# A decoder layer on one core: all steps ordered by a string of letters, first expert tiles in three parts, routing batch by batch

## What is computed

```python
x = _layernorm(x + _attn(x, x, x, ..., True), ln1_g, ln1_b)
x = _layernorm(x + _attn(x, encoder_output, encoder_output, ..., False), ln2_g, ln2_b)
x = _layernorm(x + _moe(x, router_w, router_b, e_w1, e_b1, e_w2, e_b2), ln3_g, ln3_b)
# _attn
scores = jnp.einsum('bqhd,bkhd->bhqk', Q, Kp) / jnp.sqrt(jnp.float32(HD))
a = jax.nn.softmax(scores, axis=-1)
o = jnp.einsum('bhqk,bkhd->bqhd', a, V).reshape(Bq, Sq, Dm)
# _moe
topw, topi = jax.lax.top_k(softmax(xf @ rw + rb), K)
h = gelu(einsum('td,edf->etf', xf, w1) + b1[:, None, :], approximate=False)
out = einsum('etd,te->td', einsum('etf,efd->etd', h, w2) + b2[:, None, :], combine)
```

## Time and profile before

| | |
|---|---|
| median of three runs | 1112.58 us (1112.13 to 1116.31) |
| the profiled execution: time, span | 1113.5 us, 1111.8 us |
| TensorE matmuls busy | 1020.5 us, 92% |
| ScalarE, VectorE, GpSimd busy | 588.8 us, 562.8 us, 306.6 us |
| mean granted TensorE clock | 0.971 |
| chain that ended last: TensorE, ScalarE, VectorE, DMA | 80%, 6%, 5%, 4% |

### The profile page before, as it was taken

The page is one execution under the profiler, slowest core; times in us unless marked ns, Lnnn a source line. Parts: engine busy times, 40 slices in busy tenths (PEclk is TensorE's granted clock), DMA queues, the critical chain, the costliest instruction groups (busy, mean ns, idle before and its releaser), DMA issues.

```text
span 1111.8 us, 19112 instructions
## 1 busy us (share of the span) xinstructions
PE 1020.5 (92%) x6320; PEld 593.4 (53%) x6321; DVE 562.8 (51%) x922; ACT 588.8 (53%) x1201; POOL 306.6 (28%) x416
## 2 busy tenths in 40 slices
PE   5899799999999999999999999996688899999976
PEld 3445445334336534344433333322678899999965
DVE  3542566876665767766775766842231121121126
ACT  2264363776765676766566666664233344433462
POOL 7633622405104712103233022361022011111114
PEclk9899999999999999999999999999789899999988
DMA  8634222004105202103503021021112053125134
GB/s 226 162 100 123 66 70 78 20 1 116 30 2 132 69 2 58 30 2 101 174 2 86 1 58 29 20 92 53 53 48 84 13 194 123 49 90 182 43 101 141
DMA packets 71650, 83.98 MB, mean 76 GB/s; under 512 B 10657, under 2 KB 65185, under 8 KB 71457
## 3 DMA queue, kind: packets, MB, share of 16 engines
q1 hardware_dynamic: 66080, 65.79, 20.9%
q0 software_dynamic: 5504, 17.34, 4.6%
HBM read 38.89 MB, written 12.36 MB: 46 GB/s over the span
## 4 chain that ended last, share of the span: by engine, by line
PE 80%; ACT 6%; DVE 5%; DMA 4%; issue 2%; SPq 2%; POOL 1%; ACTq 0%; POOLq 0%; DVEq 0%
PE o_bank L1057 15%; PE v_slot L1470 11%; PE a_bank L1042 11%; PE v_slot L1015 9%; PE a_bank L1462 9%; PE a_bank L983 6%; ACT probs L1170 4%; PE a_bank L998 3%; PE v_slot L1019 3%; PE o_bank L1462 3%; DVE max_q L1227 3%; PE v_slot L1079 2%; DMA inputs<-slots_in 2%; PE v_slot L1065 1%; PE v_slot L1020 1%
## 5 line engine op out<-in xcount | busy, mean ns | idle before, releaser
L1227 DVE TENSOR_REDUCE max_q<-v_slot 128x1 f32<-128x1024 f32 (+3 forms) x352 | 398.5, 1171 | 152.6 <-PE v_slot L1015 90.1
L1170 ACT ACTIVATE probs<-a_bank 128x512 f32<-128x512 f32 (+1 forms) x688 | 361.7, 592 | 176.7 <-PE a_bank L1042 115.8
L1042 PE MATMUL a_bank<-q_stack_cross,k_stack_cross 99*128 99x512 bf16 x512 | 165.7, 384 | 5.8 <-ACT probs L1170 4.0
L1476 ACT ACTIVATE hidden<-a_bank,b 128x128 f32<-128x128 f32 x216 | 79.2, 367 | 160.5 <-PE a_bank L1462 149.0
L1015 PE MATMUL v_slot<-k_stack_cross,q_stack_cross 96*128 96x512 bf16 x512 | 152.0, 382 | 4.0 <-DVE max_q L1227 2.9
L1057 PE MATMUL o_bank<-probs,v_cross 128*32 128x512 f32 x1024 | 136.4, 604 | 6.0 <-ACT probs L1170 3.2
L1462 PE MATMUL a_bank<-x_col,stack_or_weights 128*128 128x128 f32 x864 | 114.4, 285 | 18.7 <-ACTq L1192 15.7
L1470 PE MATMUL v_slot<-stack_or_weights,hidden 128*128 128x256 f32 x576 | 130.3, 379 | 0.0
L1462 PEld LDWEIGHTS a_bank<-x_col,stack_or_weights 128*128 128x128 f32 x864 | 110.6, 201 | 21.1 <-ACTq L1192 16.1
L1042 PEld LDWEIGHTS a_bank<-q_stack_cross,k_stack_cross 99*128 99x128 bf16 x512 | 46.5, 97 | 136.7 <-ACT probs L1170 89.7
L1470 PEld LDWEIGHTS v_slot<-stack_or_weights,hidden 128*128 128x128 f32 x576 | 106.6, 190 | 13.0
(11 more groups left out here) (237 smaller groups left out, 1153.4 us busy)
## 6 DMA issues: line engine op xcount, KB each, us to landing
stack_or_weights<-in_e_w SPq DMA_DIRECT2D x16, 1024.0 KB, 7.7
stack_or_weights<-parts SPq DMA_DIRECT2D x96, 128.0 KB, 2.4
k_stack_cross<-parts SPq DMA_DIRECT2D x96, 128.0 KB, 2.4
q_stack_cross<-parts SPq DMA_DIRECT2D x48, 128.0 KB, 2.4
inputs<-in_ctxT POOLq DMA_DIRECT2D x4, 1024.0 KB, 7.3
y_got<-token_out SPq DMA_DIRECT2D x16, 256.0 KB, 6.2
x_slots<-slots_in SPq DMA_DIRECT2D x30, 129.0 KB, 2.1
inputs<-in_xT POOLq DMA_DIRECT2D x4, 512.0 KB, 4.7
```

Of the source, the lines that this page charges most:

```text
L1042: last = nc.tensor.matmul(bank[:, i * cols:(i + 1) * cols], lhs, q_stack[kind][0:KM, G * u + j, q0:S], start=True, stop=bool(kind))
L1170: nc.scalar.activation(probs[tile % 2][:, js[0]:js[-1] + 1, q0:S], a_bank[at % AS][:, 0:len(js) * (S - q0)].rearrange("p (j t) -> p j t", ...
L1227: nc.vector.tensor_reduce(most, rows, X, ALU.max, negate=True).then_inc(v_free, 1)
L1476: nc.scalar.activation(hidden[:, f, :], h_bank[f % HB][:, 0:P], ACT.Gelu, bias=b1[:, bass.ds(e * FC + f, 1)]).then_inc(flow.gelu_done, 1)
```

## The change

1. The planner is gone. `STEPS`, a string of 1448 letters, says of which chain the next step is taken (w weigh, o o_turn, e score, m max or max_rows, r rows_in, a k v s c the chains of projections, loads and norms). The steps themselves are the same, except for routing.
2. Routing (`choose`, `place`) is done for each batch alone, in one scratch tile; `scatter` of a batch follows its `place`, one behind each `weigh`. Only batch 2's eight are left where 24 were.
3. The early tiles are in three parts: the first expert's but the last tile (behind `norm`), that last tile (behind `route`), and the second expert's (behind `rank`). `early_tiles_i` counts whole tiles, at least two. `choose` of batch 3 runs at once behind its logits; what counts the tiles stands behind the second expert's first tile; the wait for the last early store stands behind the first rows of flow `main`.
4. SyncE loads the weights that are needed later (`more_loads`) behind the first four splits, with `b1` among them; `b2` stays behind the early rows. The padding rows share memory with `y_self` and are made on GpSimd (`pads`) late. The last cross norm's gamma and beta go to GpSimd.

```diff
+STEPS = (
+    "aavavammmmmmkammmrkmmammkvememrmemeeemwmeeemeweawwmmmreemeemeemeewmeeweweemeweraeaeweeoeeweweweeeoeoeeweeemmwmememwwmoasm"
...
+    "wocccccc")
...
+            if b < B - 1:
+            c_chain += [("choose", b), ("place", b)]
...
+        if ev == ("split", 0, 3):
+            spread.append(("more_loads",))
+        if ev == ("max_parts", 3):
+            spread.append(("add_bias", 0))
+        if ev[0] == "place":
+            rows += [("scatter", ev[1] * QT + t, k) for t in range(QT) for k in range(2)]
+        if ev[0] == "weigh" and rows:
+            spread.append(rows.pop(0))
...
+    for step, behind in ((("pads",), ("choose", B - 2)), (("first_row",), ("att_turn", B - 1, 1)), (("experts", 0), ("norm", B - 1, 1)), (("experts", 1), ("route", B - 1)),
+                         (("rank",), ("experts", 1)), (("experts", 2), ("rank",))):
...
             sp.wait_ge(v_free, NO.v["o_turn", len(UNIT_LIST) - 1] + 1)
-            sp.dma_start(b1[:, :], a["e_b1"]).then_inc(moe_const, 16)
             sp.dma_start(b2[:, :, :], a["e_b2"].rearrange("(o e) n -> o e n", o=1).to_broadcast([P, E, D])).then_inc(moe_const, 16)
...
-                    if e == 0:
+                    part = ev[1]
+                    if part == 0:
                         sc.wait_ge(early_ready, 1)
-                        sc.wait_ge(moe_const, 32)
+                        sc.wait_ge(b1_in, 16)
...
-                        dve.wait_ge(moe_const, 32)
+                        dve.wait_ge(moe_const, 16)
 
                         dve.wait_ge(v_free, NO.v["out", B - 1, 1] + 1)
                         dve.sem_inc(early.y_evac, 1)
-                    expert_tiles(dve, early, e, lambda g, i: finish_tile(dve, early, e, g))
+                    if part < 2:
+                        early_part(dve, part, lambda g: finish_tile(dve, early, expert_of(part), g))
+                    else:
+
+                        finish_tile(dve, early, 1, first_of_second(dve))
+                        count_tiles(dve)
+                        early_part(dve, 3, lambda g: finish_tile(dve, early, 1, g))
...
+            dve.wait_ge(early.y_evac, count + 1)
+            dve.sem_inc(main.y_evac, 1)
             dve.wait_ge(early.row_ready, count + 2)
-            dve.wait_ge(early.y_evac, count + 1)
-            dve.wait_ge(early.y_stored, count * 16)
-            dve.sem_inc(main.y_evac, 1)
             copy_row(dve, main, 0)
             copy_column(dve, main, 0)
             copy_row(dve, main, 1)
+            dve.wait_ge(early.y_stored, count * 16)
```

More of the change, by code:

```diff
@@ L402, in place @@
-        if k == "split" and ev[2] == 9:
-            self.held["o_t"] = None
-    def flush_sp(self, now):
-        left = []
-        for ready, ev in sorted(self.todo_sp, key=lambda x: x[0]):
-            guard = 0.0
-            b, kind, u = UNIT_LIST[ev[1]]
-            if b:
-                guard = self.done.get(("weigh", UNIT_NO[b - 1, kind, u], key_tiles(kind) - 1))
-            if guard is None or max(ready, guard) > now:
-                left.append((ready, ev))
-                continue
-            self.order.append(ev)
-            self.done[ev] = self.use("sp", max(ready, guard), 700) + ROWS_LAND
-        self.todo_sp = left
@@ L420, in step @@
-    def step(self):
-        now = self.free["pe"]
-        self.flush_sp(now)
-        heads = []
-        for name, track in self.tracks.items():
-            i = self.at_head[name]
-            if i < len(track):
-                ready = self.needs(track[i])
-                if ready is not None:
-                    heads.append((name, track[i], ready))
-        if not heads:
-            times = [max(r, 0.0) for r, _ in self.todo_sp]
-            assert times, ("nothing can follow", self.order[-5:])
-            self.free["pe"] = max(now, min(t for t in times if t > now) if any(t > now for t in times) else now + 500)
-            return
-        first = min(max(r, now) for _, _, r in heads)
-        near = [h for h in heads if max(h[2], now) <= first + self.SOON]
-        name, ev, ready = min(near, key=self.rank)
-        self.at_head[name] += 1
-        self.place(ev, ready)
@@ L467 @@
-ORDER = Planner().build()
+            if n == UNIT_NO[B - 1, 0, UNITS - 1] and kt == QT - 1:
+                order.append(("experts_in",))
+            if kt == key_tiles(UNIT_LIST[n][1]) - 1:
+                order.append(("o_out", n))
+        elif k == "stats" and ev[2] == 0 and ev[1] + 1 < B:
+            order.append(("load_res", ev[1] + 1))
+        elif k == "norm" and ev[2] == 0 and ev[1] + 1 < B:
+            order.append(("add_bias", ev[1] + 1))
+    assert all(at[letter] == len(track) for letter, track in tracks.items())
@@ L470 @@
+    return order
+ORDER = in_order()
 class Numbers:
@@ L907, in attention_gpsimd @@
                     nc.gpsimd.tensor_tensor(rstd[:, :], rstd[:, :], neg_half[:, :], ALU.pow).then_inc(rstd_ready, 1)
-                elif k == "norm" and not on_vector(*ev[1:]):
+                elif k == "norm":
                     b, kind = ev[1:]
@@ L1372, in decoder_layer @@
         prob_step = sb("prob_step", [P, TT])
-        gelu_warm = sb("gelu_warm", [P, 1])
         top_w = sb("top_w", [P, 2, TT])
```

564 lines of the change are left out of this document (171 added, 393 removed).

## The result

| | before | after |
|---|---|---|
| median of 5 runs each, us | 1112.58 | 1048.88 |
| profiled execution, us | 1113.50 | 1043.74 |
| its span, us | 1111.8 | 1042.0 |
| mean granted clock | 0.971 | 0.984 |

The ratio is **0.9412**, with a 95% interval of 0.9385 to 0.944: faster by 63.7 us, against 60.5 foretold (1052, range 1034 to 1080). The profiled execution of after is the shortest of its five, so its own difference (69.8 us) is some 6 us too kind; where it matters, the same stretch of other runs with the same order stands beside it.

What follows compares the result with a forecast made beforehand. TensorE was taken to set the time, with about 73 us lost between its matmuls in attention. Gains of 34 + 2 + 15.1 + 4.4 + 5 = 60.5 us gave 1052 us, range 1034 to 1080.

Steps and rivals of the forecast that it cites:

- What bounds it: Whole kernel: TensorE sets the time; the order can only give back what it loses between its matmuls.
- The term of attention, 34 us: First max to last weigh: the new order gives back 34 us of the 73 lost; bounds 10 and 49.
- the haircut: Attention: only 34 of the full 47 us taken, for uncounted queue collisions and crumbs another order may not remove.
- The sum itself: Attention: TensorE work missing between dependent steps, summed along the list; 70.5 us before, 26 now, trusted as measure of loss.
- The opening, 2 us: Start: stacks loaded first bring the first max 5 us earlier, less 3.5 for two value steps; net 2 (0 to 5).
- Last weigh to second product, 15.1: Last weigh to first expert tile: earlier table load and row loads start its second product at 778.7, not 793.76.
- Last route, 4.4: Around the last route: second product to second product falls from 17.8 to 12.0 us, less one loop entry; 2 to 6.
- Early to main, 5: Early to main tiles: 16.2 us becomes 10.4, gaining 5.8 at full clock, 3.5 if half clock stays; 5 taken.
- C: Rival on the tail: early rows come as late as before, 15.1 becomes 5.5, total 1062; chance 0.10.
- A: Rival on attention: the order gives only 10 us, as GpSimd and SyncE stall in line, total 1076; chance 0.17.
- D: Rival: slower than before, 1117 to 1149, as SyncE's in-order queue is held at each of 32 rows_in; chance 0.03.
- B: Rival: missing work is the whole truth, 49 + 5 in attention and opening, 27 behind, total 1032; chance 0.11.

Runs made afterwards that it cites:

- x_opt: Changed kernel with another order of the same letters, found by lowering the sums of missing work between dependent steps; 1109.85 us, ratio 0.9976.
- x_old: Changed kernel with the attention steps in the order of the kernel before, everything else as changed; 1099.73 us, ratio 0.9884.
- x_load: Changed kernel with the later weights back at the head of SyncE's queue, ahead of the first split's stacks; 1063.99 us, ratio 0.9482.
- x_place: Changed kernel with the last two routing steps (choose and place of batch 2) five weighs later in the list; 1054.03 us, ratio 0.9469.
- x_two: Changed kernel with the first early expert's last tile ahead of the last route step, not behind it; 1064.52 us, ratio 0.9482.
- x_yst: Changed kernel with VectorE's wait for the last early store back ahead of the main part's first row copies; 1059.75 us, ratio 0.9447.
- x_best: Changed kernel with the result bank given back earlier, b2 awaited only ahead of the evacuation, and an order moved along the queues' measure; 1061.55 us, ratio 0.9463.

## Why the prediction was right, point by point

- **What bounds it.** Right. TensorE sets the time, and what it lost between its matmuls was there to be had. Its busy time would have hidden a part: idle time in the middle fell by only 7.1 us.
- **The term of attention, 34 us: too small by 9 to 13.** Attention and opening together gave 47 to 52 us, with 4 to 5 for the loads of the opening, so 43 to 47 for the order. The last weigh, foretold at about 727, came at 711.6 (714 to 716 in the three kernels like it). The step that failed is the haircut ("crumbs that another order may not remove"): TensorE's idle time in the middle went from 8.4 to 1.3 us, and both reasons given, GpSimd and SyncE in line, are not seen in it (they are in x_opt). The full value of the sum, 47, would have met it.
- **The sum itself, though, was not the measure I took it for.** It met the loss of two orders (70.5 for 73, 26 for about 24) and fell on the four built to test it, also without what three of these lost in the opening. Which waits make up the 43 to 47 us is therefore not shown; that the order as a whole does is (x_old). That it "agrees with the 73 us lost" was no proof: those two orders differ in all terms at once. That the forecast's attention came as near as it did is in part luck. The queues followed in order give 51 for the same change.
- **The opening, 2 us: right in its first part, the rest open.** The 2 us were 5 for the loads less 3.5 for two value steps that now stand behind the first max. The loads gave 4 to 5. What the value steps cost no run prices: x_load and x_old leave their places as they are, so their cost lies within the 43 to 47 us of the order.
- **Last weigh to second product, 15.1: right** (14.2), with its parts: the table load beside `out`, a stop of 3.23 us for `b2` (2.5 foretold), loads that began 15 us before the last weigh. Only the half clock behind the stop was missed, 1.8 us.
- **Last route, 4.4: right.** 17.8 to 12.5 us is 5.3. That the size fits is in part luck: the two loop entries of 1.4 us each are not seen (the second product behind them stands 7.38 us on, against 7.25 within a loop); instead the tile behind the route runs at half clock in part and takes 5.5 us to its second product, where 3.8 stood in the sum.
- **Early to main, 5: wrong, it is 1.** The sum of 10.4 us came out as 14.9. Two steps of it failed. The first half was put at full clock, 3.8 us, and took 6.7 at half clock: 2.9 of the 4.5 missing. And "now it follows the evacuation": VectorE's copy starts 1.8 us behind the start of the evacuation (789.41 and 791.25), where 0.6 stood; 1.2 more. The bound "if that stays, 3.5" was no lower end. The prediction also weighed that the shorter gap may keep the full clock (the Trainium skill, "TensorE: Matmul & The Clock Gate", What's actually happening); here it did not, the granted clock from 787 to 800 us is 0.74.
- **The rivals.** C had its place right (x_place prices late rows at 8.8 us) and did not occur, A and D neither; B, the full value, is what attention did, and the small terms of the tail brought the total back.

So that the total came within 3.2 us is luck: 11 to 16 us too few for attention and opening met 6 too many behind them. The profile's 69.8 shows the larger remainder, and the median's 63.7 the smaller.

## What to carry to other kernels

A static count of distances between dependent steps can say that an order is better, but do not tune to it: follow each engine's queue from the first step to the last, all of them, and expect a resolution of some 10 us in 700. A measure that agrees with two kernels which differ in everything has been tested once, not once for each of its terms; raise one term alone and run it, and look in the trace whether something else moved with it, as the opening did here. In the tail look for which landing ends last and who is queued behind it: a bank that is free can be given back before an engine waits for something else.

## What the runs showed of the hardware that I had not expected

Half clock came behind short stops too, and not behind all of them. After and x_two stop for 3.23 and 3.05 us ahead of the first second product and lose clock behind it; x_yst stops there for 1.08 us and x_load for 1.09, and they do not. The stretch behind it in after (PEclk is the third number from the end):

```profile
728.00:732.00 4.00, 4.00 (x12) 3.21 (x13) 2.54 (x4) 0.00 (x0) 3.85 (x3) 0.57 0.02 4
```

In x_two:

```profile
741.00:745.00 4.00, 3.86 (x11) 3.16 (x12) 2.49 (x4) 0.00 (x0) 3.92 (x2) 0.63 0.01 4
```

In x_yst:

```profile
738.00:742.00 4.00, 3.54 (x16) 3.15 (x17) 3.73 (x6) 0.00 (x0) 2.50 (x2) 1.00 0.01 4
```

Such drops also part runs of the same order: after and x_yst both have one behind the first max, x_yst has a second one at 49.0 us, and the copy of its first unit stands at 59.01 where after has it at 56.72.

All four kernels of the last chip, and none of the others, show a stop in the first tile of the second early expert or just behind it: ScalarE stands for 8.40 us in x_yst (8.44 in x_load, 8.38 in x_best, twice 2.5 in x_two), with nothing in the profile that it waits for but "remote", and TensorE 3.71 us behind it. What it is stays open. The timeline of x_yst:

```profile
781.97 0.88 ACT L1234 ACTIVATE hidden<-a_bank,b 128x128 f32<-128x128 f32 x3 [8.40 <-remote]
782.39 2.50 PE L1220 MATMUL a_bank<-x_col,stack_or_weights 128*128 128x128 f32 x12 [3.71 <-ACT hidden L1234]
```
